# An order of its own per engine for the set-up of batch 0, with the bias sums as rows and x in two transfers, in a fused perceiver block (cross-attention, self-attention, mixture of experts) on one core

## What is computed

```python
x = x + xattn(layernorm(x), ctx_1024)      # ctx_1024: 4 x 2048 x 512
x = x + attn(layernorm(x))                 # 16 heads of 32, rotary
x = x + ffn(x)                             # 8 experts, 2 per token

def xattn(x, context):
    xn = layer_norm(x, g1, b1)
    cn = layer_norm(context, g2, b2)
    q, k, v = xn @ Wq.T, cn @ Wk.T, cn @ Wv.T        # 16 heads of 32
    scores = einsum("bqhs,bkhs->bhqk", q, k) / sqrt(32)
    return einsum("bhqk,bkhs->bqhs", softmax(scores), v) @ Wo.T + bo
```

## Time and profile before

| | us |
|---|---|
| median of 3 runs (1050.6 to 1055.69) | 1051.71 |
| the profiled execution | 1052.48 |
| its span in the profile | 1050.7 |
| TensorE busy in the span | 910.6 |
| VectorE, ScalarE, GpSimd busy | 686.8, 525.5, 399.4 |

### The profile page before, as it was taken

How to read it: one execution, slowest core, us unless ns; L and a number is a source line. 1 busy time by engine, 2 the same in 40 slices (tenths; PEclk the granted TensorE clock), 3 DMA queues, 4 the chain that set the end, 5 groups by cost and what they waited for, 6 DMA issues and landing times. The chain is left out here.

```text
span 1050.7 us, 24415 instructions
## 1 busy us (share of the span) xinstructions
PE 910.6 (87%) x10361; PEld 623.1 (59%) x10361; DVE 686.8 (65%) x1001; ACT 525.5 (50%) x794; POOL 399.4 (38%) x297
## 2 busy tenths in 40 slices
PE   4787999999999999999999999766885408999996
PEld 4455666757756756766766766543443306777764
DVE  4764578656678545577654444884767473999993
ACT  2432444454444454444454354351545505999983
POOL 1120367435656345566445455532321150122112
PEclk9869999999999999999999999869987757999999
DMA  9333211333311341221341121006700329899993
GB/s 329 85 93 112 63 38 31 97 105 80 103 48 29 90 136 51 59 55 35 114 126 38 44 62 41 22 1 195 329 1 1 124 82 364 333 404 401 398 364 41
DMA packets 48487, 134.56 MB, mean 128 GB/s; under 512 B 10030, under 2 KB 11822, under 8 KB 44538
## 3 DMA queue, kind: packets, MB, share of 16 engines
q1 hardware_dynamic: 45580, 126.97, 35.7%
q0 software_dynamic: 2800, 6.04, 2.8%
HBM read 94.93 MB, written 11.33 MB: 101 GB/s over the span
## 5 line engine op out<-in xcount | busy, mean ns | idle before, releaser
L400 POOL TENSOR_TENSOR acc_pool<-acc_pool,pT 128x1024 f32<-128x1024 f32 x92 | 216.7, 2355 | 170.5 <-ACT pT L649 168.9
L507 DVE TENSOR_REDUCE mpart<-ps_b 128x1 f32<-128x512 f32 x256 | 175.1, 686 | 101.0 <-PE ps_b L786 100.0
L649 ACT ACTIVATE pT<-ps_s 128x1024 f32<-128x1024 f32 x128 | 130.7, 1021 | 215.6 <-PE ps_s L808 215.5
L770 PE MATMUL ps_a<-wv_hi,cT_hi 128*128 128x128 f16 x1024 | 186.2, 221 | 0.0
L772 PE MATMUL ps_a<-wv_hi,cT_lo 128*128 128x128 f16 x1024 | 185.0, 220 | 0.0
L771 PE MATMUL ps_a<-wv_lo,cT_hi 128*128 128x128 f16 x1024 | 184.9, 220 | 0.0
L502 DVE TENSOR_TENSOR k_lo<-k_f,k_hi 128x512 f16<-128x512 f32 x64 | 71.6, 1119 | 68.6 <-ACT k_hi L633 68.3
L786 PE MATMUL ps_b<-k_stack,q_stack 98*128 98x512 f16 x256 | 98.7, 386 | 12.8 <-DMA k_stack<-k_lo 7.4
L770 PEld LDWEIGHTS ps_a<-wv_hi,cT_hi 128*128 128x128 f16 x1024 | 100.4, 98 | 12.0 <-issue 11.9
L808 PE MATMUL ps_s<-q_stack,k_stack 98*128 98x128 f16 x1024 | 98.5, 224 | 8.0 <-ACT pT L649 7.7
L771 PEld LDWEIGHTS ps_a<-wv_lo,cT_hi 128*128 128x128 f16 x1024 | 100.9, 99 | 5.9
(11 more groups left out here) (235 smaller groups left out, 1861.3 us busy)
## 6 DMA issues: line engine op xcount, KB each, us to landing
w_raw<-in_w SPq DMA_DIRECT2D x30, 2048.0 KB, 13.8
raw<-in_context SPq DMA_DIRECT2D x16, 1024.0 KB, 5.7
k_stack<-k_hi SPq DMA_DIRECT2D x256, 64.0 KB, 2.0
k_stack<-k_lo SPq DMA_DIRECT2D x128, 64.0 KB, 2.0
slots_in<-a_zeros SPq DMA_DIRECT2D x1, 3855.0 KB, 14.0
rows_in<-slots_in SPq DMA_DIRECT2D x15, 257.0 KB, 12.0
q_stack<-k_stack SPq DMA_DIRECT2D x12, 128.0 KB, 2.3
x_sb<-in_x SPq DMA_DIRECT2D x4, 256.0 KB, 3.5
```

The lines of the kernel that those rows point to most:

```text
L400: nc.gpsimd.tensor_tensor(acc_pool[:, :], pT[:, 0, :] if p == 1 else acc_pool[:, :], pT[:, p % PT, :], ALU.add).then_inc(pool_add, 1)
L507: nc.vector.tensor_reduce(mpart[:, j, kb:kb + 1], bank_b(step)[:, :], AX.X, ALU.max).then_inc(p1_max, 1)
L649: nc.scalar.activation(pT[:, p % PT, :], ps_s[:, :], ACT.Exp, scale=SM_SCALE).then_inc(exp_done, 1)
L770: nc.tensor.matmul(to, cT_hi[:, c, keys], t.wv_hi[:, c, col], start=(c == 0), stop=False)
```

## The change

Each engine gets a list of its own for the set-up, in a table of words (`x0`: transposes of x for batch 0; `t5`: tile 5; `k1`, `v2`: key or value block of window 0; `n0` to `n2`: key blocks of window 1; `p0` to `p15`: the maxima of window 0; the others as above). A bias is now 4 float32 matmuls with the shift vector as the stationary operand (one column) and the weights moving (512 columns); ScalarE copies this row to partition 0 of `acc_pool` and 4 small matmuls turn it into a column (step "col"). Value weights are loaded and folded before key weights. x comes in two transfers of 512 KB. Four of the twelve copies of the second half of k_stack for window 0 are issued by ScalarE.

```diff
-    steps = [("xs",)] + tiles("st", 0) + [("xn",)] + tiles("nm", 0) + [("bias", 0)]
...
-    return steps + [("mt", 0)] + block(1, 2) + [("s", 0, 0, 0), ("s", 0, 0, 1)]
+SET_UP = {
+    "PE": "x0 x1 x2 x3 bias0 t0 t1 col0 q0 t2 t3 q1 t4 t5 bias2 q2 q3 col2 bias1 t6 t7 col1 v0 k0 t8 t9 k1 t10 "
+          "t11 v1 t12 t13 v2 t14 t15 k2 k3 p0 p1 v3 p2 p3 n0 p4 p5 n1 p6 p7 p8 p9 p10 p11 p12 p13 p14 p15 mt s n2",
...
+    "SP": "t3 q3 t7 t11 mask k1 t15 k3 n1",
+}
...
-            for b in range(NB):
-                sp.dma_start(t.x[:, b, :], io.x[b:b + 1, :, :].rearrange("b t c -> (b t) c")).then_inc(x_in[b], 16)
+            for n in range(2):
+                sp.dma_start(t.x[:, 2 * n:2 * n + 2, :], io.x[2 * n:2 * n + 2, :, :].rearrange("b t c -> t b c")
+                             ).then_inc(x_in[n], 16)
...
+            sp.dma_start(w_raw[2], chunked(io.wvT)).then_inc(w_in[2], 16)
             sp.dma_start(w_raw[1], chunked(io.wkT)).then_inc(w_in[1], 16)
             load(0, 2)
+            load(0, 3)
             sp.dma_start(mask_u8[:, :], io.mask).then_inc(mask_u8_in, 16)
-            sp.dma_start(w_raw[2], chunked(io.wvT)).then_inc(w_in[2], 16)
-            load(0, 3)
...
+                        if (w, h, k) == (0, 1, 1):
+                            continue
...
+                    if (w, kb) == (0, NKB - 1):
+
+                        act.wait_ge(placed, PLACED)
+                        act.wait_ge(mask_rows_out, 48)
+                        act.wait_ge(k_hi_out, NKB)
+                        for j in range(HPG):
+                            act.dma_start(t.k_stack[0][HD:2 * HD, j, 2 * KB:4 * KB], k_hi[1][HD * j:HD * (j + 1), :]
+                                          ).then_inc(k_in[0][1], 16)
...
+            def bias_in_a_row(i):
+                n = BIASES.index(i)
+                pe.wait_ge(w_in[i], 16)
+                if n:
+                    pe.wait_ge(row_out, n)
+                for c in range(NC):
+                    last = nc.tensor.matmul(ps_a[0][0:1, :], vectors[:, 2 + min(i, 1), c:c + 1], w_raw[i][:, c, :],
+                                            start=(c == 0), stop=(c == NC - 1))
+                last.then_inc(bias_mm, 1)
+
             def bias_columns(i):
-
-                pe.wait_ge(w_in[i], 16)
-                if i:
-                    pe.wait_ge(bias_out, i)
+                n = BIASES.index(i)
+                pe.wait_ge(row_out, n + 1)
+                if n:
+                    pe.wait_ge(bias_out, n)
                 for g in range(NG):
-                    for c in range(NC):
-                        last = nc.tensor.matmul(bias_bank[:, NG * i + g:NG * i + g + 1],
-                                                w_raw[i][:, c, P * g:P * (g + 1)],
-                                                vectors[:, 2 + min(i, 1), c:c + 1], start=(c == 0), stop=(c == NC - 1))
-                last.then_inc(bias_mm, 1)
+                    last = nc.tensor.matmul(ps_a[1][:, NG * n + g:NG * n + g + 1], bias_row[n][:, P * g:P * (g + 1)],
+                                            t.ident[0:1, 0:1], start=True, stop=True)
+                last.then_inc(col_mm, 1)
```

More of the change, by code:

```diff
@@ L111, in window_steps, with set_up @@
     return steps
-def first_steps():
+SET_UP = {
[9 rows of a table added]
+}
+def set_up(engine):
     def tiles(kind, n):
@@ L121, in block, with all_steps @@
         return [("k", w, kb, c) for c in range(NC)]
-    def values(q):
-        return [("v", 0, q, i) for i in range(QUAD)]
-    side = [("p1", 0, j, kb) for h in range(2) for j in range(HPG) for kb in (2 * h, 2 * h + 1)]
-    steps = [("xs",)] + tiles("st", 0) + [("xn",)] + tiles("nm", 0) + [("bias", 0)]
[L128 to L135, removed]
-    return steps + [("mt", 0)] + block(1, 2) + [("s", 0, 0, 0), ("s", 0, 0, 1)]
-def all_steps():
-    steps = first_steps()
+    maxima = [("p1", 0, j, kb) for h in range(2) for j in range(HPG) for kb in (2 * h, 2 * h + 1)]
+    steps = []
+    for word in SET_UP[engine].split():
+        kind = word.rstrip("0123456789")
+        n = int(word[len(kind):] or 0)
+        steps += {"st": lambda: tiles("st", n), "nm": lambda: tiles("nm", n), "t": lambda: [("t", 0, n)],
+                  "k": lambda: block(0, n), "n": lambda: block(1, n), "v": lambda: [("v", 0, n, i) for i in range(QUAD)],
+                  "p": lambda: [maxima[n]], "x": lambda: [("xt", n)], "mt": lambda: [("mt", 0)],
+                  "s": lambda: [("s", 0, 0, 0), ("s", 0, 0, 1)], "q": lambda: [("q", n)], "fold": lambda: [("fold", n)],
+                  "bias": lambda: [("bias", n)], "col": lambda: [("col", n)]}.get(kind, lambda: [(kind,)])()
+    return steps
+def all_steps(engine):
+    steps = []
     for w in range(WINDOWS):
         steps += window_steps(w)
-    return steps + [("den", WINDOWS - 1), ("low", WINDOWS - 1)] + [("op", NB - 1, n) for n in range(NG)]
+    steps += [("den", WINDOWS - 1), ("low", WINDOWS - 1)] + [("op", NB - 1, n) for n in range(NG)]
+    return set_up(engine) + (halves_behind_maxima(steps) if engine == "DVE" else steps)
 def halves_behind_maxima(steps):
@@ L173, in cross_attention @@
 def cross_attention(nc, io, t, s):
-    steps = all_steps()
+    steps = all_steps("PE")
     ring_a = [step[:3] for step in steps if step[0] in ("k", "v", "op") and step[-1] == 0]
@@ L248, in cross_attention @@
         split_hi, split_lo = sem("split_hi"), sem("split_lo")
-        x_in, ident_in = [sem(f"x_in{b}") for b in range(NB)], sem("ident_in")
+        x_in, ident_in = [sem(f"x_in{n}") for n in range(2)], sem("ident_in")
         w_in, vec_in, bo_in = [sem(f"w_in{i}") for i in range(4)], sem("vec_in"), sem("bo_in")
@@ L275, in x_bank @@
             return (ps_s[:, 0:KB], ps_s[:, KB:2 * KB], ps_o[0][:, :], ps_o[1][:, :])[b]
-        bias_bank = ps_a[1]
+        BIASES = (0, 2, 1)
+        bias_row = [acc_pool[0:1, KB * (n % 2):KB * (n % 2 + 1)] for n in range(3)]
         def bank_a(step):
@@ L321, in place_queries @@
                         sp.dma_start(heads[:, j, :, :], part[HD * j:HD * (j + 1), :, :]).then_inc(placed, 16)
-            for step in steps:
+            for step in all_steps("SP"):
                 if step == ("q", NG - 1):
@@ L385, in _ @@
             n_add = 0
-            for step in steps:
+            for step in all_steps("POOL"):
                 if step[0] == "st" and step[2] % 2 == 1:
@@ L441, in queries_statistics @@
                 for b in range(NB):
-                    v.wait_ge(x_in[b], 16)
+                    v.wait_ge(x_in[b // 2], 16)
                     nc.vector.bn_stats(x_stats[:, b, :], t.x[:, b, :]).then_inc(x_st, 1)
@@ L471, in _ @@
             ends_added = [0]
-            for step in halves_behind_maxima(steps):
+            for step in all_steps("DVE"):
                 kind = step[0]
@@ L594, in _ @@
             act.wait_ge(gains_done, 3)
-            for step in steps:
+            for step in all_steps("ACT"):
                 kind = step[0]
@@ L605, in _ @@
                 elif kind == "bias":
+                    bias_row_out(step[1])
+                elif kind == "col":
                     bias_columns_out(step[1])
@@ L616, in _ @@
                     act.wait_ge(v_mm, NQ * w + q + 1)
+                    if w == 0 and q == 0:
+                        act.wait_ge(w_lo, 3)
                     nc.scalar.activation(vals[w % 2][:, QUAD * q:QUAD * (q + 1), :].rearrange("p k n -> p (k n)"),
@@ L731, in _ @@
                 elif kind == "bias":
+                    bias_in_a_row(step[1])
+                elif kind == "col":
                     bias_columns(step[1])
@@ L748, in _ @@
                         if w == 0:
-                            pe.wait_ge(w_lo, 2)
-                        if w == 0 and kb == 1:
+                            pe.wait_ge(w_lo, 3)
                             pe.wait_ge(bias_out, 3)
@@ L765, in _ @@
                         if w == 0:
-                            pe.wait_ge(w_lo, 3)
+                            pe.wait_ge(w_lo, 2)
+                            pe.wait_ge(bias_out, 3)
                     kt, col = QUAD * q + i, slice(P * g, P * (g + 1))
```

17 lines of the change are left out of this document (12 added, 5 removed), and 6 rows, old and new, of the table SET_UP.

## The result

| | us |
|---|---|
| forecast (range) | 1030.6 (1025 to 1037) |
| after, median of 4 runs (1034.14 to 1040.78) | 1035.88 |
| before, median of 4 runs beside them | 1052.29 |
| ratio after / before, 95% interval | 0.9848 (0.9804 to 0.9891) |
| the profiled execution of after, its span | 1040.78, 1039.0 |

The change saves 16.4 us (1052.29 - 1035.88), where 21.1 were forecast. The profiled execution is the slowest of the four. The same kernel ran again in later sessions: the second gave 1036.37 (6 runs, ratio 0.9853, 0.9831 to 0.9875), two single runs 1032.38 and 1034.5. All twelve have a median of 1035.3 and spread from 1032.4 to 1041.5. That spread is part of the answer.

A forecast was written before the change was run, and what follows sets the result against it. TensorE was taken as the bound, so the landmark's shift passes to the end: 70.8 work + 21.6 idle + 5.5 clock = 97.9 us, 21.1 earlier than 119.0, giving 1030.6 us, range 1025 to 1037.

The forecast's parts named there:

- the landmark: First value matmul of window 1, at 119.01 us before; forecast at 97.9, 21.1 earlier, passing through to the end.
- First wait: TensorE's wait at the program's start, until x is normalised: 9.8 us forecast, 13.38 before.
- query 0: TensorE's wait ahead of query 0 for the low part of Wq: 1.6 us forecast where 4.9 stood.
- tiles 12 and 13: TensorE's wait there, since their normalisation runs beside GpSimd's sum on x: 1.4 us forecast.
- the maxima: Ten maxima in a row, TensorE waiting for VectorE's reductions of 0.70 us each: 6.2 us idle forecast.
- Tile 3's 1.1: Tile 3 waits for tile 1's low half, behind the statistics of tiles 4 to 7: 1.1 us forecast.
- I count none: Wait of the maxima for the copies into k_stack, 4.0 us before at the second half: put at nothing.
- rival B: SP's chain of loads, mask row and copies for k_stack's first half ends late: 1033 to 1035 us; chance 0.12.
- Rival C: The 512-column bias rows cost 1.7 us each, so 5.3 less in all: 1025.3 us; chance 0.08.
- I count one of the two: Clock falls at query 0's wait or the ten maxima, one counted: 2.8 + 2.7 = 5.5 us, bounds 2.8 and 8.2.
- rival A: Low clock lasts longer, at both open places and around small gaps between them: 1036 to 1040 us; chance 0.12.
- both open places: Where a clock fall was left open: the 1.6 us wait at 18.8 and the ten maxima; a fall costs 2.7.

The follow-up runs named there:

- the third execution: The changed kernel unaltered, a single later profiled run beside no other change: 1032.38 us, landmark 99.03.
- the first execution: The changed kernel itself, the profiled execution of its first four runs: 1040.78 us, landmark 102.97.
- the second: The changed kernel unaltered, run again beside the kernel before: median 1036.37 us (6 runs), profiled execution 1032.75, landmark 98.97.
- the run with four: Kernel before, with normalised x ahead of the statistics of tiles 0 to 3, x's transposes ahead of the first bias, x still in four transfers: 1048.12 us.
- the run with both repairs and the keys left in place: Changed kernel with the mask row ahead of loads in SP's list and maxima interleaved with quarters of v3, n0, n1, n2; keys unmoved: 1028.68 us.
- the rows alone: Kernel before, in its old order, with bias sums as rows and x in two transfers: 1054.83 us, ratio 1.0038.
- rows within the new order: Judged by the changed kernel with the old one-column bias form put back where the rows stand: 1038.84 us, ratio 0.9867.
- keys first: Changed kernel with mask row first, maxima interleaved, k2 between tiles 13 and 14 and k3 ahead of v2: 1031.3 us, ratio 0.9783.

## Why the prediction was right, and what it missed

**The bound and the direction.** Right. The windows within a batch keep their length (for example 35.15 and 35.89 us from one row product to the next, in both traces), so the shift of the landmark passes on: in the third execution 20.0 us at the landmark, 20.1 at the span's end (1050.7 to 1030.6).

**Idle time: right to 0.7 us, with one term missing.** First wait 9.8, measured 9.9; query 0 1.6 and 1.6; value block 0 0.6 and 0.4; tiles 12 and 13 1.4 and 1.1, with 0.5 ahead of tile 4 that was not forecast. For the maxima, from maximum 6 at 82.61 to the row product at 90.65 are 8.04 us with 2.2 of work at the full clock: 5.85 idle for 6.2; the scores 0.7 for 0.9. Tile 3's 1.1 is not there in the first execution and 0.9 in the second. Sum without the copies 20.05 for 21.6. The term put at nothing, the wait for the copies into k_stack, was 2.2. The step that failed is "I count none": it looked at the second half, and the wait came at the first, where rival B had it. B's reason was the right one: the chain of loads, row and copies ends at 70.25, beside maximum 0. It put 2.4 to 4.4 us on the forecast, for dearer issues and a load ahead, and named neither SP's wait of 5.0 for tile 11 nor the 5.0 of the row; the wait is 2.2, and where the clock falls behind it 1.8 more.

**Work.** A bias row was put at 3.5 us and lasts 3.59 where the clock is up, a column 0.9 and lasts 1.05. The clock's loss in the first bias of before was taken as 3.5, and its rows give 3.3 (6.96 less 3.63). So 70.8 forecast, and 102.97 - 22.25 (idle) - 9.5 (clock) = 71.2 found. Rival C is out: the row lasts 3.59 us, not 1.7. Two transfers for x changed nothing, as assumed (first wait 9.9, and 9.8 in the run with four).

**The clock: the term that was mis-sized.** "I count one of the two." The first execution lost about 9.5 us: 2.0 at the start, 1.6 in query 0, 1.8 behind the wait at maximum 0 and 4.1 from the row product to the end of n2. These are durations at the low level less those at the high one: 1.87 for 1.03 in the row product, 0.63 for 0.38 in a matmul of n2 (0.42 for 0.215 from start to start). The second lost 98.97 - 22.3 - 71.2 = 5.5, by the same idle time and work: 2.7 at the start and 2.8 behind the maxima, as forecast. So 5.5 is what the clock costs in its better executions, and the forecast took one outcome of a quantity that varies by 4 us for its value. The first execution is what rival A said, a fall at both open places, and its time, 1040.78, lies at the upper end of A's 1036 to 1040. So A happens in some executions of the kernel and not in others, where the prediction had it as one outcome or the other. Of the maxima it can be said that they make it fall each time (four executions of four); of query 0 twice in four; of maximum 0 once in four, at a gap of 2.2 that left it up in two others.

**The end.** The time less the landmark was 933.5 us before (1052.48 - 119.01). In the changed kernel it is 937.8, 933.8, 933.4 and 934.5, in the other variants up to 941.6; the four with a landmark under 94 have 936.0 to 940.3. Part of that is the turn from one batch to the next (window 10 to 11 lasts 45.09 before and 48.15 in the first execution); part lies in the 120 us behind the last row copy, where TensorE is not the bound and its clock varies. The window of before:

```profile
683.10:803.10 120.00, 83.00 (x688) 46.96 (x686) 82.89 (x112) 49.09 (x152) 32.24 (x33) 0.86 0.32 115
```

And of the run with both repairs and the keys left in place, whose landmark was 25.1 us earlier and its end only 18.2 (1050.7 - 1032.5):

```profile
658.40:778.40 120.00, 87.77 (x688) 47.73 (x686) 77.11 (x106) 48.65 (x149) 30.53 (x32) 0.81 0.32 115
```

The same 688 matmuls take 4.8 us more, at a lower clock. The gain at the landmark (19 to 20 us in three executions of four) is larger than that of the medians (16.4 and 16.2). But those three executions, at 1032.4 to 1034.5, are also among the fastest of the twelve, and they keep their gain to the end; an execution near the median is not among the traces, so where it loses 1 to 3 us more, ahead of the landmark or behind it, is not shown. In the four profiled executions the forecast, which carried its 21.1 unchanged to the end, was too large by 1.1 to 5.1 us at the landmark and by 0 to 4 behind it. Whether an earlier start itself makes these stages longer, or it is chance in fourteen profiles, stays open.

**Where the 16 us come from.** x first 4.4; the rows alone 0; rows within the new order about 4; so the order of the rest some 8 to 12, by difference and not measured alone. The exchange of key and value weights has no run of its own.

## What to carry to other kernels

Ask of each gap in TensorE's work two prices: its length, and what the work behind it costs at half the clock. Breaking up ten small matmuls that wait on VectorE gave 5 us at the landmark, more than taking away the wait for a DMA did (1.3). Of a small transfer whose result is needed, ask what stands ahead of it in its issuer's list: here a load that itself waited 5.0 us for another engine, and then slowed the row. And a repair that only makes one engine earlier is given back at the next hand-over: bias rows in the old order gave nothing, and keys first put a wait of 2.9 us ahead of key block 3.

## What the runs showed of the hardware

- A float32 matmul with one stationary column and 512 moving takes 0.9 us (two instructions of 0.45 each; four matmuls in 3.59). A float16 matmul of 512 columns takes 0.215 from start to start, so each instruction takes about twice that.
- Executions of one kernel with waits alike differ by 4.0 us at the landmark through the clock alone.
- A gap of 2.2 us let the clock fall in one execution and not in two others of the same kernel.
- The mask's row (16 KB, written to memory) was there 2.0 us after its issue when it was issued ahead of a load of 1 MB, and 5.0 us after it right behind one.
